# The last stage's attention rewritten: mask in PSUM, values spread ahead of the loop, two pairs of groups in work

## The chip, the cores and the metric

The kernel runs on one core of a Trainium2 chip. The metric is the device time of one execution in microseconds (us). Engines are named as the profile names them: PE is the matrix engine (PEld its weight loads), DVE the vector engine, ACT the scalar engine, POOL is GpSimd, SP issues the DMAs.

## What is computed

The reference is a two-layer perceiver with six blocks on `x` of 32 batches x 64 tokens x 128 (B, T, D). Only the last block is touched by the change. Seen by that block, S is the first axis (32, so the batches) and B the second (64, the tokens): attention runs over the 32 entries of the first axis, causally, separately for each of the 64 tokens, with 16 heads of 8 numbers and 4 key heads, each shared by 4 query heads.

```python
def _L1_ffn_ref(hidden_states, ln1_weight, ..., moe_w1, moe_w2):   # hidden_states = _layernorm(x)
    ln1_out = _layernorm(hidden_states, ln1_weight, ln1_bias)
    qkv = jnp.einsum('sbh,oh->sbo', ln1_out, qkv_weight)           # 16 query, 4 key, 4 value heads of 8
    k, v = jnp.repeat(k, 4, axis=2), jnp.repeat(v, 4, axis=2)
    scores = jnp.einsum('sbhd,tbhd->bhst', q, k) * scale
    scores = jnp.where(causal, scores, jnp.finfo(scores.dtype).min)
    probs = jax.nn.softmax(scores, axis=-1)
    attn = jnp.einsum('bhst,tbhd->sbhd', probs, v).reshape(S, B, H)
    hidden_after_attn = hidden_states + jnp.einsum('sbh,oh->sbo', attn, proj_weight)
    ln2_out = _layernorm(hidden_after_attn, ln2_weight, ln2_bias)
    ... # top 2 of 8 experts, F = 256, gelu
    return hidden_after_attn + moe_out
x = x + _L1_ffn_ref(_layernorm(x), ...)
```

## The kernel before

The program is a row of stages, each a block with one instruction list per engine, written out by hand with semaphores; a stage begins when the one before it has ended on all engines. The change is in the last stage but the final store, `stage_ffn1`. `x` lies in SBUF as 16 tiles (NT) of 128 rows; in the stages before, tile n holds 128 consecutive rows of (batch, token).

**Entry.** SP stores `x` to the output tensor, waits for it, and loads it back by token with four DMAs (`by_token`), so that partitions 32q to 32q+31 of tile n hold the 32 batches of token 4n+q; then it issues ten loads of weights. DVE waits for the reload (`ldx`), runs the first layer norm (`norm_vector`: L196 statistics, L199, L201, a power on POOL at L217, L205 the subtraction and scaling of each tile), then the second norm with gain and shift (L209, L211). PE transposes the result (L229), ACT copies it to `hT` (L237). PE makes queries and keys (L2640, L2641), which ACT copies to `QT` and `KT` (L2540, L2542), and the values of all tiles (L2643), which DVE copies to `V` (L2572).

**Loop.** A group g is one tile: 4 tokens, all 16 heads. The loop takes a pair of groups per turn, 8 turns, and an iteration starts with the scores of its own pair. Per group:

- POOL spreads the keys over heads (L2521: 128x2048 numbers, `kx`) and the values over the 4 tokens (L2526, `vx`); ACT copies the queries (L2548, `qs`).
- PE: scores, 4 matmuls on 32 columns of the array each, 512 wide (L2653).
- DVE: mask added (L2580, reads PSUM), maximum (L2583), subtraction (L2586), ACT the exponential (L2551), DVE the sum (L2590), reciprocal (L2593), multiplication (L2596), 32x32 transposes (L2600, `PT`).
- PE: probabilities times values for all heads and all key heads (L2660, 512 wide); DVE keeps the right key head (L2603), adds over key heads (L2608), transposes (L2611).
- PE transposes (L2665), ACT copies (L2555), PE projects (L2668), DVE adds to `hn` (L2614).

Buffers are double (`[a]` with a = g mod 2), and each engine goes through the steps for both groups of the pair before the next step. After the loop DVE adds `hn` to `x` (L2617), the third norm follows, the routing and the experts (`Moe`, L1356, L1365, L1383, L1397).

## Time and profile before

| | us |
|---|---|
| median of 3 runs | 3585.48 (3583.09 to 3586.24) |
| time of the profiled execution | 3584.38 |
| its span | 3582.6 |
| last stage, from the first DMA of `x` (3189.80) to the end | 392.8 |
| of it: until POOL's first key spread (3247.09) | 57.3 |
| of it: the 8 pairs, to the last add into `hn` (3427.30) | 180.2 |
| of it: from there to the end | 155.3 |

The profiled execution's time is 1.8 us above its span and 1.1 us below the median. A time such as 3247.09 is counted from the span's start. PE's fp32 matmuls stand in the records as two instructions each (x8 for 4 matmuls).

### The profile page before, as it was taken

The numbers are of one execution on the slowest core, as the hardware profiler recorded it, in microseconds if no ns is written. First come the engines' busy times: TensorE is split into PE (matmuls) and PEld (weight loads), VectorE is DVE, ScalarE is ACT, GpSimd is POOL, SyncE is SP. The second block draws the span as 40 slices with busy tenths as digits, with TensorE's granted clock in tenths as the row PEclk, the third lists the DMA queues.
The fourth block names the chain that finished last, engine by engine and source line by source line (L and its number), as shares of the span: only waits on it lengthen the run. The fifth ranks groups of instructions, "written<-read, shape, count | busy, mean of one in ns | idle before, by whom it ended". The sixth has DMA issues, their size and how long they took to land. (4 is left out here: it accounts for less than half of the span.)

```text
span 3582.6 us, 61448 instructions
## 1 busy us (share of the span) xinstructions
PE 3029.7 (85%) x19468; PEld 1775.1 (50%) x19468; DVE 2220.2 (62%) x4759; ACT 1464.9 (41%) x2290; POOL 1968.8 (55%) x1270
## 2 busy tenths in 40 slices
PE   4799999999995789958999999999994888834368
PEld 2455555555553767723444444444442777721146
DVE  4577777777774541156767767767736666545753
ACT  2466666666662223344444444444432121101123
POOL 2577777788775300026888888888870333323300
PEclk8899999999997899978999999999996999966679
DMA  5655555555530010010000000000000000020000
GB/s 171 165 187 190 188 180 178 182 186 186 188 139 3 0 48 0 0 43 19 28 27 23 23 27 27 18 27 27 19 0 8 1 0 0 0 52 0 0 1 12
DMA packets 143131, 230.56 MB, mean 64 GB/s; under 512 B 15683, under 2 KB 80779, under 8 KB 143052
## 3 DMA queue, kind: packets, MB, share of 16 engines
q1 hardware_dynamic: 143052, 229.55, 19.9%
q8 instruction: 44, 0.72, 0.1%
q14 instruction: 35, 0.29, 0.0%
HBM read 147.03 MB, written 82.47 MB: 64 GB/s over the span
## 5 line engine op out<-in xcount | busy, mean ns | idle before, releaser
L432 POOL TENSOR_TENSOR sb_a_acc<-sb_a_acc,sb_a_PT 128x1024 f32<-128x1024 f32 x256 | 604.4, 2361 | 36.7 <-ACT sb_a_PT L510 29.5
L593 DVE TENSOR_REDUCE sb_a_mx<-ps_a_A 128x1 f32<-128x512 f32 x768 | 506.4, 686 | 97.7 <-PE ps_a_A L752 92.6
L510 ACT ACTIVATE sb_a_PT<-ps_a_SC 128x1024 f32<-128x1024 f32 (+1 forms) x416 | 425.8, 1024 | 314.1 <-PE ps_a_SC L775 274.1
L1649 POOL TENSOR_TENSOR sb_a_acc<-sb_a_acc,sb_a_PT 128x512 f32<-128x512 f32 (+2 forms) x384 | 487.7, 1270 | 38.5 <-ACT sb_a_PT L1741 12.5
L1741 ACT ACTIVATE sb_a_PT<-ps_a_SC 128x1024 f32<-128x1024 f32 (+2 forms) x256 | 234.3, 916 | 561.2 <-PE ps_a_SC L2012 327.3
L2028 PE MATMUL ps_a_PV<-sb_a_PT,sb_a_XN 128*128 128x512 f32 (+2 forms) x896 | 433.1, 600 | 0.0
L1836 DVE TENSOR_REDUCE sb_a_mx<-ps_a_A 128x1 f32<-128x512 f32 x384 | 256.1, 679 | 266.0 <-PE ps_a_A L1987 265.6
L2012 PE MATMUL ps_a_SC<-sb_a_QX,sb_a_XT 128*128 128x512 f32 (+1 forms) x832 | 397.3, 597 | 0.0
L752 PE MATMUL ps_a_A<-sb_a_KS,sb_a_QS 97*128 97x512 bf16 x768 | 301.6, 393 | 24.1 <-DVE sb_a_QS L585 18.2
L786 PE MATMUL ps_a_PV<-sb_a_PT,sb_a_V 128*32 128x256 f32 (+1 forms) x3328 | 267.3, 393 | 5.6 <-ACT sb_a_PT L510 5.2
L775 PE MATMUL ps_a_SC<-sb_a_QS,sb_a_KS 105*128 105x128 bf16 (+1 forms) x3328 | 257.7, 220 | 13.4 <-DVE sb_a_QS L607 13.4
L775 PEld LDWEIGHTS ps_a_SC<-sb_a_QS,sb_a_KS 105*128 105x128 bf16 (+1 forms) x3328 | 218.1, 99 | 84.3 <-ACT sb_a_PT L510 23.2
L2012 PEld LDWEIGHTS ps_a_SC<-sb_a_QX,sb_a_XT 128*128 128x128 f32 (+1 forms) x832 | 152.6, 186 | 203.4 <-issue 200.4
L2028 PEld LDWEIGHTS ps_a_PV<-sb_a_PT,sb_a_XN 128*128 128x128 f32 (+2 forms) x896 | 163.1, 190 | 129.7 <-issue 116.6
L973 POOL TENSOR_TENSOR sb_a4c_LT<-sb_a4c_E,sb_LV 128x512 f32<-128x512 f32 x48 | 66.6, 1394 | 285.7 <-DVE sb_a4c_QL L1002 224.2
L217 POOL TENSOR_TENSOR sb_rstd<-sb_rstd,sb_half 128x16 f32<-128x16 f32 x8 | 23.2, 2906 | 350.0 <-DVE sb_rstd L201 350.0
L432 POOL TENSOR_TENSOR sb_a_acc<-sb_a_PT 128x1024 f32<-128x1024 f32 x32 | 75.4, 2357 | 227.3 <-ACT sb_a_PT L510 227.3
L1611 POOL TENSOR_TENSOR sb_a_XN<-sb_a_C,sb_a_gm 128x1536 f32<-128x1536 f32 x64 | 123.4, 1951 | 92.7 <-PE ps_a_PV L2028 89.3
L1830 DVE TENSOR_SCALAR sb_a_C<-sb_a_C,sb_a_cag,sb_a_crs 128x128 f32<-128x128 f32 (+1 forms) x416 | 170.7, 483 | 2.6 <-POOL sb_a_crs L1604 2.6
L752 PEld LDWEIGHTS ps_a_A<-sb_a_KS,sb_a_QS 97*128 97x128 bf16 x768 | 74.6, 97 | 175.0 <-DVE sb_a_mx L593 110.4
L1022 DVE TENSOR_TENSOR sb_a4c_XX<-sb_a4c_XX,ps_a4c_PP 128x1024 f32<-128x1024 f32 (+1 forms) x80 | 89.1, 1113 | 113.1 <-PE ps_a4c_PP L958 113.1
L1987 PE MATMUL ps_a_A<-sb_a_XTb,sb_a_QXb 128*128 128x512 bf16 x384 | 137.3, 386 | 16.3 <-DVE sb_a_mx L1836 16.3
(526 smaller groups left out, 5914.2 us busy)
## 6 DMA issues: line engine op xcount, KB each, us to landing
sb_a_C<-in_ctx_dram SPq DMA_DIRECT2D x64, 768.0 KB
...
sb_a_KS<-a_KD SPq DMA_DIRECT2D x256, 192.0 KB
...
sb_a_KS<-a_KD SPq DMA_DIRECT2D x256, 108.2 KB
...
```

Source lines behind the costliest of these rows:

```text
L432: pool.tensor_tensor(acc[:, :], first[:, :], PT[slot(a, j)][:, :], ALU.add).then_inc(s["acc"], 1)
L510: act.activation(PT[slot(a, j)][0:n, :], SC[(a + j) % 2][0:n, :], ACT.Exp).then_inc(s["exp"], 1)
L593: v.tensor_reduce(mx[:, p, c:c + 1], A[u % 2][:, :], AXX, ALU.max).then_inc(s["am"], 1)
L752: mm = pe.matmul(A[u % 2][:, :], QS[a][0:ROWM + 1, p, :], KS[a][0:ROWM + 1, p, 512 * c:512 * c + 512], start=True, stop=True)
L775: mm = pe.matmul(SC[(a + j) % 2][0:m, P * p:P * p + P], KS[a][0:ROWS, p, P * j:P * j + m], QS[a][0:ROWS, p, :], start=True, stop=True)
L786: mm = pe.matmul(PV[32 * g:32 * g + 32, 0, :], V[a][0:m, j, 32 * g:32 * g + 32], PT[slot(a, j)][0:m, G * T * g:G * T * g + G * T], start=( ...
L1649: pool.tensor_tensor(acc[a][0:m, :], first, PT[u % 4][0:m, HQ * i:HQ * i + HQ], ALU.add).then_inc(s["acc"], 1)
L1741: act.activation(PT[u % 4][0:m, 0:n], SC[u % 2][0:m, 0:n], ACT.Exp).then_inc(s["exp"], 1)
L1830: v.tensor_scalar(C[a][0:m, j, :], C[a][0:m, j, :], cag[a][0:m, j, 0:1], crs[a][0:m, j:j + 1], ALU.subtract, ALU.mult)\
L1836: v.tensor_reduce(mx[:, u % 4, u // 4:u // 4 + 1], A[u % 2][:, :], AXX, ALU.max).then_inc(s["am"], 1)
L2012: mm = pe.matmul(o, XT[a][:, col(j):col(j) + m], QX[a][:, :, :], start=True, stop=True)
L2028: mm = pe.matmul(PV[:, :], XN[a][0:m, j, :], PT[u % 4][0:m, HQ * i:HQ * i + HQ], start=(j == 0), stop=(j == NK))
```

## The change

**Entry.** `x` is stored as before, but DVE no longer waits for a reload: the first norm runs on `x` in its old order. The weights are issued right behind the store. When the first norm is done, SP stores `hn` to a scratch tensor and loads it by token into `HP`; `x` itself is reloaded by token after that. The second norm also runs in the old order; the reordering to tokens is made by ACT's copy into `hT`, whose writes are now 32 numbers apart, and PE's query and key matmuls wait for all four of these copies. DVE makes two small bf16 copies, the mask for 16 heads (`cmb`) and four unit matrices side by side (`rep4`).

**Values.** POOL clears a tile `vx` of 8192 numbers per partition between the powers of the first and the second norm. DVE writes the values into it from PSUM with 4 instructions, one per key head, each head's 8 numbers at their own place among 32 columns. V's copy and POOL's 16 spreads go.

**Loop.** POOL spreads 10 heads of the keys, ACT the other 6, with one instruction each; `kx` has four buffers, so both can be 4 groups ahead. ACT's copy of the queries goes. The mask enters the scores by a bf16 matmul over 32 rows that starts the accumulation, so DVE takes the maximum and the subtraction straight from PSUM. The exponentials are transposed undivided; the product with the values is made per key head, 16 matmuls of 128 columns into one 128-wide result, which needs no selection of key heads; DVE transposes it from PSUM and multiplies by the reciprocal sums there. The loops are unrolled.

```diff
+    HP = sb("HP", [P, NT, D])
+    HD = nc.dram_tensor("a5_HD", (B * T, D), F32, kind="Internal").ap()
...
+    vx = sb("vx", [P, NT, Q4, KVH, KD])
+    kx = [sb(f"kx{i}", [P, Q4, H, B]) for i in range(4)]
...
-            sp.wait_ge(s["st"], 16)
-            by_token = d["out"].rearrange("b (n q) d -> q b n d", q=Q4)
-            for q in range(Q4):
-                sp.dma_start(k.x[B * q:B * q + B, :, :], by_token[q]).then_inc(s["ldx"], 16)
...
+            sp.wait_ge(s["n"]["norm"], NT)
+            sp.dma_start(HD.rearrange("(n p) d -> p n d", p=P), k.hn[:, :, :]).then_inc(s["sth"], 16)
+            sp.wait_ge(s["sth"], 16)
+            by_token = HD.rearrange("(b n q) d -> q b n d", b=B, q=Q4)
+            for q in range(Q4):
+                sp.dma_start(HP[B * q:B * q + B, :, :], by_token[q]).then_inc(s["ldh"], 16)
...
+            pool.memset(vx[:, :, :, :, :], 0.0).then_inc(s["vz"], 1)
...
-            pool.wait_ge(s["vc"], 1)
-            with pool.Fori(0, NT // 2) as i:
...
-                    wait(pool, s["sc"], g - 1)
-                    pool.tensor_tensor(kx[a][:, :, :, :],
...
+            for g in range(NT):
+                wait(pool, s["sc"], g - 3)
+                pool.tensor_tensor(kx[g % 4][:, :, 0:KH, :], tok(KT, g).unsqueeze(2).to_broadcast([P, Q4, KH, B]),
+                                   k.heads[:, 0:KH].unsqueeze(1).unsqueeze(3).to_broadcast([P, Q4, KH, B]), ALU.mult).then_inc(s["kp"], 1)
...
-            norm_scalar(k, act, s["n1"], banks)
+            for c in range(NT // 4):
+                act.wait_ge(s["n1"]["turned"], c + 1)
+                act.activation(k.hT[:, :].rearrange("p (t b) -> p b t", b=B)[:, 8 * c:8 * c + 8, :],
+                               banks[c % 2][:, :].rearrange("p (b t) -> p b t", t=T), ACT.Copy).then_inc(s["n1"]["copied"], 1)
...
+            def spread(g):
+
+                wait(act, s["sc"], g - 3)
+                for h in range(KH, H):
+                    act.activation(kx[g % 4][:, :, h, :], tok(KT, g), ACT.Identity, scale=k.heads[:, h:h + 1]).then_inc(s["ka"], 1)
...
-            v.wait_ge(s["ldx"], 16 * Q4)
...
+            v.wait_ge(s["cm"], Q4 + 1)
+            v.tensor_copy(cmb[:, :, :], cmask[0:B, :].unsqueeze(1).to_broadcast([B, H, B])).then_inc(s["cb"], 1)
+            v.tensor_copy(rep4[:, :, :], k.ident[0:B, 0:B].unsqueeze(1).to_broadcast([B, Q4, B])).then_inc(s["cb"], 1)
...
-            v.tensor_copy(flat(V), LG[:, :]).then_inc(s["vc"], 1)
...
-                    v.tensor_tensor(Sm[a][:, :, :], hb(SB[a]), cmask[:, :].unsqueeze(1).to_broadcast([P, H, B]), ALU.add).then_inc(s["dm"], 1)
...
-                    v.tensor_tensor(Sm[a][:, :, :], Sm[a][:, :, :], mm_[a][:, :].unsqueeze(2).to_broadcast([P, H, B]), ALU.subtract)\
...
-                    v.tensor_tensor(Sm[a][:, :, :], Sm[a][:, :, :], mm_[a][:, :].unsqueeze(2).to_broadcast([P, H, B]), ALU.mult)\
...
-                    v.tensor_tensor(Om[a][:, :, :].rearrange("p (k h) q -> p k (h q)", k=KVH),
...
-                    v.tensor_reduce(R[a][:, :], Om[a][:, :, :].rearrange("p (k h) q -> p (h q) k", k=KVH), AXX, ALU.add).then_inc(s["r1"], 1)
...
+                cs = slice(DH * c, DH * c + DH)
+                v.tensor_tensor(vx[:, :, :, c, cs], values[:, :, cs].unsqueeze(2).to_broadcast([P, NT, Q4, DH]),
+                                k.quad[:, :].unsqueeze(1).unsqueeze(3).to_broadcast([P, NT, Q4, DH]), ALU.mult).then_inc(s["vc"], 1)
...
+            def tops(g):
+                wait(v, s["sc"], g + 1)
+                v.tensor_reduce(top[g % 2][:, :], hb(SB[g % 2]), AXX, ALU.max).then_inc(s["dx"], 1)
...
+            def less(g):
+                wait(v, s["dx"], g + 1)
+                v.tensor_tensor(Sm[g % 2][:, :, :], hb(SB[g % 2]), top[g % 2][:, :].unsqueeze(2).to_broadcast([P, H, B]), ALU.subtract)\
...
+            def sums(g):
+                wait(v, s["ex"], g + 1)
+                wait(v, s["nr"], g - 1)
+                v.transpose(flat(PT[g % 2]), flat(Sm[g % 2])).then_inc(s["pt"], 1)
+                v.tensor_reduce(sum_[g % 2][:, :], Sm[g % 2][:, :, :], AXX, ALU.add).then_inc(s["su"], 1)
...
+            def turn(g):
+                wait(v, s["pv"], g + 1)
+                v.transpose(R[g % 2][:, :], OB[g % 2][:, 0:P]).then_inc(s["r2"], 1)
...
+            def normalise(g):
+                wait(v, s["r2"], g + 1)
+                wait(v, s["rc"], g + 1)
+                r = R[g % 2][:, :].rearrange("p (h k d) -> p h k d", h=4, k=KVH)
+                by = sum_[g % 2][:, :].rearrange("p (k h) -> p h k", k=KVH).unsqueeze(3).to_broadcast([P, 4, KVH, DH])
+                v.tensor_tensor(r, r, by, ALU.mult).then_inc(s["nr"], 1)
...
+            def add(g):
+                wait(v, s["pr"], g + 1)
+                v.tensor_tensor(HP[:, g, :], HP[:, g, :], banks[g % 2][:, P:2 * P], ALU.add).then_inc(s["hx"], 1)
...
+            for i in range(NT // 2):
+                now, then = (2 * i, 2 * i + 1), [g for g in (2 * i + 2, 2 * i + 3) if g < NT]
+                for g in then:
+                    tops(g)
+                for g in then:
+                    less(g)
+                for g in now:
+                    turn(g)
+                for g in now:
+                    normalise(g)
+                for g in then:
+                    sums(g)
+                for g in then:
+                    inverse(g)
+                for g in now:
+                    add(g)
...
-            v.tensor_tensor(k.x[:, :, :], k.x[:, :, :], k.hn[:, :, :], ALU.add).then_inc(s["xh"], 1)
+            v.wait_ge(s["ldx"], 16 * Q4)
+            v.tensor_tensor(k.x[:, :, :], k.x[:, :, :], HP[:, :, :], ALU.add).then_inc(s["xh"], 1)
...
-                pe.wait_ge(s["n1"]["copied"], c + 1)
+                pe.wait_ge(s["n1"]["copied"], NT // 4)
...
+            def scores(g):
+                wait(pe, s["kp"], g + 1)
+                wait(pe, s["ka"], (H - KH) * (g + 1))
+                wait(pe, s["ds"], g - 1)
+                o = SB[g % 2]
+                pe.matmul(o[:, :], rep4[:, :, :], cmb[:, :, :], start=True, stop=False)
+                q = tok(QT, g)
+                for t in range(Q4):
+                    mm = pe.matmul(o[B * t:B * t + B, :], q[:, t, :], kx[g % 4][:, t, :, :], start=False, stop=True)
+                mm.then_inc(s["sc"], 1)
+
+            def products(g):
+                wait(pe, s["pt"], g + 1)
+                wait(pe, s["r2"], g - 1)
+                for c in range(KVH):
                     for t in range(Q4):
-                        mm = pe.matmul(SB[a][B * t:B * t + B, :], qs[a][:, B * t:B * t + B], kx[a][:, t, :, :], start=True, stop=True)
-                    mm.then_inc(s["sc"], 1)
-                for a, g in gs:
-                    wait(pe, s["pt"], g + 1)
-                    wait(pe, s["vx"], g + 1)
...
+                        mm = pe.matmul(OB[g % 2][B * t:B * t + B, 0:P], vx[:, g, t, c, :], PT[g % 2][:, 4 * c:4 * c + 4, :],
+                                       start=(c == 0), stop=(c == KVH - 1))
+                mm.then_inc(s["pv"], 1)
...
+                wait(pe, s["nr"], g + 1)
+                wait(pe, s["zc"], g - 1)
+                pe.transpose(banks[g % 2][:, 0:P], R[g % 2][:, :], k.ident[:, :]).then_inc(s["zt"], 1)
+
+            def project(g):
...
+            for i in range(NT // 2):
+                now = (2 * i, 2 * i + 1)
+                for g in now:
+                    products(g)
+                for g in (2 * i + 4, 2 * i + 5):
+                    if g < NT:
+                        scores(g)
+                for g in now:
+                    turn(g)
+                for g in now:
+                    project(g)
```

PE in the loop before, from an iteration's first scores to its end (`sb_a_qs`, `sb_a_kx` queries and keys, `sb_a_PT` probabilities, `sb_a_R` the turned result, `sb_a_zs` its copy):

```order
L2653 MATMUL ps_a5m_U<-sb_a_kx,sb_a_qs 32x512 x4
L34 REGISTER_ALU x2
L2653 MATMUL ps_a5m_U<-sb_a_kx,sb_a_qs 32x512 x4
L2660 MATMUL ps_a5m_U<-sb_a_PT,sb_a_vx 32x512 x8
L2665 MATMUL ps_a5m_D<-sb_ident,sb_a_R 128x128 x2
L2668 MATMUL ps_a5m_D<-sb_a_WpT,sb_a_zs 128x128 x2
L2646 REGISTER_ALU
L2646 COMPARE_AND_BRANCH
```

PE in the loop of the change, from the last two scores of one turn to the first scores of the next:

```order
L2701 MATMUL ps_a5m_U<-sb_a_cmb,sb_a_rep 128x512
L2704 MATMUL ps_a5m_U<-sb_a_kx,sb_a_QT 32x512 x4
L2701 MATMUL ps_a5m_U<-sb_a_cmb,sb_a_rep 128x512
L2704 MATMUL ps_a5m_U<-sb_a_kx,sb_a_QT 32x512 x4
L2719 MATMUL ps_a5m_D<-sb_ident,sb_a_R 128x128 x2
L2724 MATMUL ps_a5m_D<-sb_a_WpT,sb_a_zs 128x128 x2
L2712 MATMUL ps_a5m_U<-sb_a_PT,sb_a_vx 32x128 x32
L2701 MATMUL ps_a5m_U<-sb_a_cmb,sb_a_rep 128x512
L2704 MATMUL ps_a5m_U<-sb_a_kx,sb_a_QT 32x512 x4
```

The scores of the pair after the next now stand between the products and the transposes of this pair, each behind its mask matmul; a pair's products are 32 matmuls of a quarter of the width, where they were 8.

DVE in the loop before, one iteration up to the second transposes:

```order
L2580 TENSOR_TENSOR sb_a_Sm<-ps_a5m_U,sb_a_cmask 128x512
L34 REGISTER_ALU
L2580 TENSOR_TENSOR sb_a_Sm<-ps_a5m_U,sb_a_cmask 128x512
L2583 TENSOR_REDUCE sb_a_mm<-sb_a_Sm 128x16 x2
L2586 TENSOR_TENSOR sb_a_Sm<-sb_a_Sm,sb_a_mm 128x512 x2
L2590 TENSOR_REDUCE sb_a_mm<-sb_a_Sm 128x16 x2
L2593 RECIPROCAL sb_a_mm<-sb_a_mm 128x16 x2
L2596 TENSOR_TENSOR sb_a_Sm<-sb_a_Sm,sb_a_mm 128x512 x2
L2600 STREAM_TRANSPOSE sb_a_PT<-sb_a_Sm 128x512 x2
L2603 TENSOR_TENSOR sb_a_Om<-ps_a5m_U,sb_subhead 128x512 x2
L2608 TENSOR_REDUCE sb_a_R<-sb_a_Om 128x128 x2
L2611 STREAM_TRANSPOSE sb_a_R<-sb_a_R 128x128 x2
```

DVE in the loop of the change, one whole turn:

```order
L2610 TENSOR_REDUCE sb_a_top<-ps_a5m_U 128x16 x2
L2614 TENSOR_TENSOR sb_a_Sm<-ps_a5m_U,sb_a_top 128x512 x2
L2629 STREAM_TRANSPOSE sb_a_R<-ps_a5m_U 128x128 x2
L2636 TENSOR_TENSOR sb_a_R<-sb_a_R,sb_a_sum 128x128 x2
L2620 STREAM_TRANSPOSE sb_a_PT<-sb_a_Sm 128x512
L2621 TENSOR_REDUCE sb_a_sum<-sb_a_Sm 128x16
L2620 STREAM_TRANSPOSE sb_a_PT<-sb_a_Sm 128x512
L2621 TENSOR_REDUCE sb_a_sum<-sb_a_Sm 128x16
L2625 RECIPROCAL sb_a_sum<-sb_a_sum 128x16 x2
L2640 TENSOR_TENSOR sb_a_HP<-sb_a_HP,ps_a5m_D 128x128 x2
```

Gone are the mask's addition, the multiplication of 128x512, the selection and the sum over key heads; the maximum and the subtraction of the next pair now stand ahead of this pair's transposes, and the add into `HP` is last.

POOL from the norms' powers into the loop, before:

```order
L217 TENSOR_TENSOR sb_rstd<-sb_rstd,sb_half 128x16 x2
L2517 UNCONDITIONAL_BRANCH
L2517 ISA
L2521 ISA
L2521 TENSOR_TENSOR sb_a_kx<-sb_a_KT,sb_heads 128x2048
L34 REGISTER_ALU
L2521 ISA
L2521 TENSOR_TENSOR sb_a_kx<-sb_a_KT,sb_heads 128x2048
L2526 ISA
L2526 TENSOR_TENSOR sb_a_vx<-sb_a_V,sb_quad 128x128
```

POOL from the block's first instruction to its last, in the change (x16 are all 16 groups):

```order
L2520 MEMSET sb_a_cmask 128x32
L2523 AFFINE_SELECT sb_a_cmask<-sb_a_cmask 32x32 x4
L217 TENSOR_TENSOR sb_rstd<-sb_rstd,sb_half 128x16
L2527 MEMSET sb_a_vx 128x8192
L217 TENSOR_TENSOR sb_rstd<-sb_rstd,sb_half 128x16
L2532 TENSOR_TENSOR sb_a_kx<-sb_a_KT,sb_heads 128x4x320 x16
L217 TENSOR_TENSOR sb_rstd<-sb_rstd,sb_half 128x16
```

The clearing of `vx` stands directly behind the power of the first norm; in the loop only the key spreads are left.

## Rows read from the trace of the kernel before

**Rows 1.** Windows of the last stage: entry and loop; columns in the first row.

```profile
core 0: us, PE busy (x) PEld busy (x) DVE busy (x) ACT busy (x) POOL busy (x), PEclk, DMA share, GB/s
3189.80:3247.10 57.30, 16.21 (x68) 10.84 (x68) 22.80 (x103) 8.30 (x18) 6.75 (x8) 0.59 0.31 81
3247.10:3427.30 180.20, 69.00 (x304) 19.31 (x304) 123.27 (x176) 17.62 (x46) 67.19 (x32) 0.60 0.00 0
```

**Rows 2.** Timeline of the loop, one iteration (its scores start at 3297.55).

```profile
3297.55 3.64 PE L2653 MATMUL ps_a5m_U<-sb_a_kx,sb_a_qs 128*32 128x512 f32 x16
3299.70 7.67 POOL L2521 TENSOR_TENSOR sb_a_kx<-sb_a_KT,sb_heads 128x2048 f32<-128x2048 f32 x2 [6.41 <-PE ps_a5m_U L2653]
3301.87 1.27 DVE L2583 TENSOR_REDUCE sb_a_mm<-sb_a_Sm 128x16 f32<-128x512 f32 x2
3303.06 4.86 DVE L2586 TENSOR_TENSOR sb_a_Sm<-sb_a_Sm,sb_a_mm 128x512 f32<-128x512 f32 x2
3309.21 0.37 DVE L2593 RECIPROCAL sb_a_mm<-sb_a_mm 128x16 f32<-128x16 f32 x2
3310.70 1.30 DVE L2600 STREAM_TRANSPOSE sb_a_PT<-sb_a_Sm 128x512 f32<-128x512 f32 x2
3317.60 0.49 DVE L2611 STREAM_TRANSPOSE sb_a_R<-sb_a_R 128x128 f32<-128x128 f32 x2
3317.96 0.56 PE L2665 MATMUL ps_a5m_D<-sb_ident,sb_a_R 128*128 128x128 f32 x2 [2.89 <-DVE sb_a_R L2611]
3318.96 0.51 ACT L2548 ACTIVATE sb_a_qs<-sb_a_QT 128x128 f32 x2
3319.60 0.29 DVE L2614 TENSOR_TENSOR sb_hn<-sb_hn,ps_a5m_D 128x128 f32 x1 [1.51 <-PE ps_a5m_D L2668]
3319.81 2.84 PE L2653 MATMUL ps_a5m_U<-sb_a_kx,sb_a_qs 128*32 128x512 f32 x16
```

**Rows 3.** Instructions of three lines: duration ns min/median/max, first and last start.

```profile
L2586 DVE TENSOR_TENSOR sb_a_Sm<-sb_a_Sm,sb_a_mm x16: 680/1638/4116, 3258.3 to 3414.0; 128x512 f32<-128x512 f32 x16
L2580 DVE TENSOR_TENSOR sb_a_Sm<-ps_a5m_U,sb_a_cmask x16: 691/692/692, 3253.0 to 3411.6; 128x512 f32<-128x512 f32 x16
L2521 POOL TENSOR_TENSOR sb_a_kx<-sb_a_KT,sb_heads x16: 3629/3634/4082, 3247.1 to 3392.5; 128x2048 f32<-128x2048 f32 x16
```

**Rows 4.** Timeline of the entry.

```profile
3202.53 3.19 DVE L196 BATCH_NORM_STATS2 sb_st<-sb_x 128x6 f32<-128x128 f32 x16 [15.93 <-DMA sb_x<-out_dram]
3210.08 4.19 DVE L205 TENSOR_SCALAR sb_hn<-sb_x,sb_mv,sb_rstd 128x128 f32<-128x128 f32 x16 [3.09 <-POOL sb_rstd L217]
3242.29 3.65 PE L2643 MATMUL ps_a_L<-sb_a_WkvT,sb_hT 128*128 128x32 f32 x32
3242.49 0.60 ACT L2542 ACTIVATE sb_a_KT<-ps_a5m_U 128x512 f32<-128x512 f32 x1 [0.26 <-PE ps_a5m_U L2641]
```

**Rows 5.** Timeline of an earlier stage's entry, with the same norm.

```profile
2701.74 7.41 DVE L205 TENSOR_SCALAR sb_hn<-sb_x,sb_mv,sb_rstd 128x128 f32<-128x128 f32 x16 [3.02 <-POOL sb_rstd L217]
2701.92 3.51 POOL L2163 MEMSET sb_a_KP<- 128x4096 f32 x1
```

**Rows 6.** Window of the entry's transfers; columns as in rows 1.

```profile
3196.00:3210.20 14.20, 0.00 (x0) 0.00 (x0) 4.55 (x34) 0.00 (x0) 2.90 (x1) 0.50 1.00 250
```

**Rows 7.** PE where passes are short, at the full clock (stages one and last).

```profile
1002.69 0.64 PE L786 MATMUL ps_a_PV<-sb_a_PT,sb_a_V 128*32 128x256 f32 x8
1003.49 0.61 PE L775 MATMUL ps_a_SC<-sb_a_QS,sb_a_KS 105*128 105x128 bf16 x8
3462.98 1.95 PE L1365 MATMUL ps_a5m_D<-sb_a_W,sb_a5m_H 128*128 128x128 f32 x16
```

**Rows 8.** Window of an earlier stage's loop; columns as in rows 1.

```profile
2800.00:2844.00 44.00, 37.87 (x271) 33.16 (x271) 28.89 (x40) 8.29 (x17) 14.18 (x10) 0.92 0.00 1
```

**Rows 9.** Groups on ACT in the stage two before: busy, mean ns, idle before.

```profile
L1700 ACT ACTIVATE sb_a_XT<-ps_a_M,sb_ident,sb_a_keep 128x512 f32<-128x512 f32 x124 | 85.0, 685 | 0.0
L1741 ACT ACT_TABLE_LOAD x1 | 1.3, 1283 | 0.0
```

More of the change, by code:

```diff
@@ L2503, in _ @@
             sp.dma_start(W2[:, :, :], d["L1_ffn_moe_w2"].rearrange("e (f p) d -> p (e f) d", p=P)).then_inc(s["ldw"], 16)
+            sp.wait_ge(s["n"]["norm"], NT)
[4 more added lines that the diff above has]
+                sp.dma_start(HP[B * q:B * q + B, :, :], by_token[q]).then_inc(s["ldh"], 16)
+            sp.wait_ge(s["st"], 16)
+            by_token = d["out"].rearrange("b (n q) d -> q b n d", q=Q4)
+            for q in range(Q4):
+                sp.dma_start(k.x[B * q:B * q + B, :, :], by_token[q]).then_inc(s["ldx"], 16)
         @block.gpsimd
@@ new lines, in inverse @@
+            def inverse(g):
+                wait(v, s["su"], g + 1)
+                v.reciprocal(sum_[g % 2][:, :], sum_[g % 2][:, :]).then_inc(s["rc"], 1)
+            def turn(g):
[7 more added lines that the diff above has]
+                v.tensor_tensor(r, r, by, ALU.mult).then_inc(s["nr"], 1)
@@ new lines, in add @@
+            def add(g):
+                wait(v, s["pr"], g + 1)
+                v.tensor_tensor(HP[:, g, :], HP[:, g, :], banks[g % 2][:, P:2 * P], ALU.add).then_inc(s["hx"], 1)
+            for f in (tops, less, sums, inverse):
+                for g in range(2):
+                    f(g)
+            v.wait_ge(s["ldh"], 16 * Q4)
+            for i in range(NT // 2):
[14 more added lines that the diff above has]
+                    add(g)
@@ new lines, in _ @@
+            pe.wait_ge(s["vc"], KVH)
+            pe.wait_ge(s["cb"], 2)
+            def scores(g):
[8 more added lines that the diff above has]
+                mm.then_inc(s["sc"], 1)
@@ new lines, in project @@
+            def project(g):
+                wait(pe, s["zc"], g + 1)
+                wait(pe, s["hx"], g - 1)
+                pe.matmul(banks[g % 2][:, P:2 * P], zs[g % 2][:, :], WpT[:, :], start=True, stop=True).then_inc(s["pr"], 1)
+            for g in range(4):
+                scores(g)
+            for i in range(NT // 2):
+                now = (2 * i, 2 * i + 1)
+                for g in now:
+                    products(g)
+                for g in (2 * i + 4, 2 * i + 5):
+                    if g < NT:
+                        scores(g)
+                for g in now:
+                    turn(g)
+                for g in now:
+                    project(g)
```

116 lines of the change are left out of this document (33 added, 83 removed).

## The prediction

> **What bounds the kernel now.** I read the page, then windows over the last stage, then the timeline of the entry and of one loop iteration, and the groups of instructions. The change lies in the last 392.8 us of a span of 3582.6; all that stands before 3189.80 stays. In the loop no engine is full: over 180.2 us DVE works 123.3, PE 69.0, POOL 67.2, ACT 17.6, with PE's granted clock at 0.60 [rows 1]. The timeline shows why. One iteration runs as a single chain: scores at 3297.55, DVE's maxima at 3301.87, subtractions, sums, transposes to 3312.0, the wide products, selection, second transposes at 3317.60, PE's transposes, ACT's copies, projections, adds, and the next scores at 3319.81. That is 22.26 us a turn, 8 times [rows 2]. Within it, two subtractions take 4.86 us instead of 1.3, because they meet POOL's key spreads (7.67 us from 3299.70): the fastest is 0.68 us, the slowest 4.12, while L2580, with one operand in PSUM, never leaves 0.69 [rows 2, 3]. So the bound is a chain of latencies with DVE as its largest member, and a rewrite gains where it shortens DVE's list and lets one pair's chain lie under another's.
>
> **The entry.** DVE's first statistics start at 3202.53, 12.7 us after the stage's start, having waited for the reload of `x`; in the change they start at about 3189.9. To the end of the last L205 (3214.27) the first norm takes 11.7 us [rows 4]. New behind its power is POOL's clearing of 8192 numbers. The trace holds the same situation once: L205's 16 instructions took 7.41 us beside a memset of 4096 numbers (3.51 us), against 4.19 without [rows 4, 5]. So the memset cost 3.2 us, nearly its whole length, and one of twice the size (7.0 us) costs between 0 and 7.0; I take 6.5. The norm then ends at 3189.9 + 11.7 + 6.5 = 3208.1. DVE next waits for the weights. Reload and weights filled the DMA engines for 14.2 us before [rows 6]; now the store of `x` stands in the reload's place from 3190.3 on, so they land by about 3204.5, hidden behind the memset. Without the memset's block the wait for them would keep all but 3.6 us.
> From L205's end to the last copy into `KT` (3243.09) it is 28.8 us [rows 4]. I add 0.7 for the two bf16 copies and 0.9 for PE's wait for all four copies into `hT` (it started after three); that these copies write 32 numbers apart has no row, 0 to 0.6 us each, and I take 0. POOL's first spread then starts at 3208.1 + 30.4 + 0.2 = 3238.7 instead of 3247.1: 8.4 us earlier. The values reach `vx` by 4 DVE instructions of about 0.61 after L2643, at 3244, so PE's first scores wait for them and not for POOL. The store of `hn`, its reload and the reload of `x` are some 3 MB at 250 GB/s [rows 6], 12 us behind PE's and DVE's preparation and loop; if that cover failed, the wait would stand ahead of the first add only.
>
> **The loop: DVE per pair.** By pace in the rows: maxima 1.2 (3301.87 to 3303.06), subtractions from PSUM 1.2, transposes 1.2, sums 1.2, reciprocals 0.3, small transposes 0.45, the two new multiplications of 128x128 at the pace of L2614 0.5, adds 0.5 [rows 2]. Sum 6.55, and 0.4 for waits between steps: 7.0 us. Gone are the mask's addition, the wide multiplication, the selection, the sum over key heads and the blocked subtraction.
>
> **PE per pair.** Sixteen records of scores, two groups, take 3.64 us at the 1.2 GHz level: four rounds of 0.855 and an end of 0.2 [rows 2]. So a group costs 1.71, or 0.85 at 2.4 GHz. The mask matmul is 512 bf16 columns; eight passes of 128 took 0.61 [rows 7], so 0.2 to 0.3, I take 0.25 (0.45 at 1.2). The new products of a group are eight rounds of four passes of 128 columns. From below they cost what the wide ones did, 0.85; two rounds of 256 columns took 0.64 with their end [rows 7], so a round of 128 lies under 0.16, and I take 0.15: 1.2 us a group. Transposes, ACT's copies and projections took 1.85 at 1.2 GHz (3317.96 to 3319.81) [rows 2], about 1.2 at 2.4. PE's turn is 2 x 1.2 + 2 x 1.1 + 1.2 = 5.8 at 2.4 GHz, under DVE's 7.0, and 2 x 1.71 + 2 x 2.16 + 1.85 = 9.6 at 1.2 GHz, over it. A loop in which PE was busy 37.87 of 44 us had a clock of 0.92 [rows 8]; the old one, busy 69 of 180, had 0.60. With 5.8 of 7.0 I expect mostly 2.4 GHz, with a third of the turns at 1.2.
>
> **ACT and POOL per pair.** ACT: 12 key spreads at the pace of two L2548 in 0.51 (0.21 each, at most 0.3), two exponentials, two copies: 4.2 to 5.3 us, hidden. Identity beside Exp needs no table load: the stage two before runs both, 124 times on L1700, with one load at its Exp [rows 9]. POOL: 1280 of 2048 numbers, 3.63 x 10/16 = 2.3 us each [rows 3], 4.6 a pair, hidden but for the lock below.
>
> **Sum.** The first turn ends late: PE has the scores of groups 4 and 5 ahead of the first transposes, and group 5's keys are POOL's sixth: 6 x 2.3 + 1.2 + 2.2 (transposes to adds) = 17.2; the first multiplication can meet a spread for 2.3 more: 19.5. Six turns of 7.0 are 42, the last 3.5: 65. A third of the turns at 1.2 GHz adds 5, the first scores at that level 2: **72 us**, between 60 and 96. The loop's end moves from 3427.3 to 3238.7 + 72 = 3310.7. The rest, 155.3, stays. Minus 116.6 from the profiled 3584.38 is 3467.8; the median of the runs is 1.1 above: **3469 us**.
>
> **Rivals.**
> - *Short passes have a floor (0.15).* Eight un-tiled passes of 128 columns took 0.61 [rows 7], 0.076 each; if 32 tiled ones cannot be closer, a group's products take 2.4 and PE's turn is 8.2: about 1.2 more on seven turns, **3477**. Against it: four tiled weight loads leave no gap between rounds now, 3.64 for four rounds of 0.855 [rows 2]. The Trainium skill, "TensorE: Matmul & The Clock Gate", section on the back-to-back issue gap, gives about 81 ns per load-and-matmul pair at 128 columns; by it a group takes 2.6, PE's turn 8.6, and the time would be 3480. No row shows it for tiled passes.
> - *PE stays at 1.2 GHz (0.14).* Turns of 9.6, fill 24, end 5: loop 87, **3484**. For it: the old loop's 0.60. Against it: at that level PE would be busy nearly always, as where the clock was 0.92.
> - *DVE waits for POOL in every turn (0.12).* The new multiplication has both operands in SBUF, like L2586. POOL's next spread starts when the scores are done, about 2.2 us after the subtraction; the multiplication stands at 1.7 to 2.2. One block a turn is 2.1 x 6 = 13, **3482**; two, or blocked transposes, 25, **3494**. Maxima beside a spread ran unblocked (1.27 for two at 3301.87), but L205, with one SBUF tensor, was blocked by a memset [rows 2, 5]; transposes beside POOL have no row. The Trainium skill, "SBUF — State Buffer", "Who interferes with whom", says that a DVE instruction with one SBUF input outside the 2-port modes does not contend; by it the transposes stay free, and only the multiplication is at risk.
> - *Column groups take turns (0.06).* 32 passes at the 0.122 of L1365 (16 in 1.95 [rows 7]) are 3.9 a group; PE's turn 11.2, **3498**.
> - *Slower (0.01).* Successive key heads add into the same PSUM columns; if each pass waited for the end of the one before (0.107 + 0.22), a group took 10.5, the turn 24.5, the loop 191: **3588**. It decides from 0.32 us a pass on. Against it: L1365 also adds twice into one place at 0.122.
> - *The memset hardly blocks (0.06).* DVE waits for the weights instead: 3465; with no turn at 1.2 GHz as well, **3458**.
>
> **Numbers.** The forecast's own case (products hidden, clock mostly high, lock rare) has 0.44, from 3458 to 3477. Range: from 3453 (fill of 17, no turn at 1.2 GHz, memset free, none of the 0.4 a turn) to 3496, which leaves out the last two costly cases and part of the third. What is left, 0.02, is code fetched for the unrolled loop and the like. This kernel can be told apart at 0.2%, 7 us; the gain is 3.2%, so faster 0.98, same 0.01, slower 0.01.
>
> **What would show it.** The first norm's statistics right at the stage's start; L205 near 10.7 us beside a memset of 7; adds into `HP` 7 us apart per pair, DVE with hardly an idle moment in the middle turns, PE's granted clock over 0.8 there; a product group of 32 records near 1.4 us. Wrong would be: records of products over 2 us a group, multiplications over 2 us, a clock near 0.5, or table loads on ACT.

## The result, and the profile of the changed kernel

The changed kernel takes 3458.27 us (median of 4 runs, 3455.61 to 3471.53) against 3585.86 (3583.09 to 3588.47) on the same chip: 0.9652 of the time, 95% interval 0.9626 to 0.9678. The forecast was 3469 (3453 to 3496). The profiled execution took 3456.78, its span is 3455.0. The windows of its last stage, entry, loop and middle turns, columns as in [rows 1]:

```profile
3186.29:3234.73 48.44, 12.74 (x45) 7.62 (x45) 28.93 (x104) 9.26 (x17) 13.59 (x9) 0.61 0.58 139
3234.73:3299.73 65.00, 54.63 (x729) 28.29 (x728) 53.46 (x132) 40.56 (x128) 37.19 (x16) 0.87 0.01 2
3257.50:3295.00 37.50, 32.66 (x532) 18.05 (x534) 37.50 (x95) 26.16 (x83) 16.25 (x7) 0.98 0.01 2
```

Against [rows 1] the entry fell from 57.3 to 48.4 us and the loop from 180.2 to 65.0; the 155.3 us behind the loop are the same. The span fell by 127.6; 3.5 of them are not the change's: all that stands before the stage, identical code, ended 3.5 us earlier in this execution. Over the loop VectorE's busy time fell from 123.3 to 53.5 us. In the middle turns it is busy in 37.50 of 37.50 us, and TensorE's granted clock is 0.98. One such turn from the timeline (start, duration, engine, line):

```profile
3270.07 0.48 DVE L2640 TENSOR_TENSOR sb_a_HP<-sb_a_HP,ps_a5m_D 128x128 f32<-128x128 f32 x2
...
3270.16 1.95 PE L2712 MATMUL ps_a5m_U<-sb_a_PT,sb_a_vx 128*32 128x128 f32 x64
3270.47 1.28 DVE L2610 TENSOR_REDUCE sb_a_top<-ps_a5m_U 128x16 f32<-128x512 f32 x2
3271.67 1.27 DVE L2614 TENSOR_TENSOR sb_a_Sm<-ps_a5m_U,sb_a_top 128x512 f32<-128x512 f32 x2
...
3272.80 1.06 PE L2704 MATMUL ps_a5m_U<-sb_a_kx,sb_a_QT 128*32 128x512 f32 x8
3272.86 0.50 DVE L2629 STREAM_TRANSPOSE sb_a_R<-ps_a5m_U 128x128 f32<-128x128 f32 x2
...
3273.29 0.45 DVE L2636 TENSOR_TENSOR sb_a_R<-sb_a_R,sb_a_sum 128x128 f32<-128x128 f32 x2
...
3273.97 4.66 POOL L2532 TENSOR_TENSOR sb_a_kx<-sb_a_KT,sb_heads 128x1280 f32<-128x1280 f32 x2 [1.63 <-PE ps_a5m_U L2704]
...
3276.35 0.49 DVE L2640 TENSOR_TENSOR sb_a_HP<-sb_a_HP,ps_a5m_D 128x128 f32<-128x128 f32 x2
```

The adds return after 6.28 us, where one iteration took 22.26 [rows 2]. Two things to see: 64 product passes (two records for each of a pair's 32 matmuls) in 1.95 us, 30 ns each; and the multiplications L2636 end at 3273.74, 0.23 us before GpSimd, released by the scores, starts its next spread. In [rows 2] the subtractions stood inside such a spread. The entry, by the same view, with the clearing beside the first norm and the first two of the regrouping copies:

```profile
3193.76 6.92 POOL L2527 MEMSET sb_a_vx<- 128x8192 f32 x1
3193.85 10.56 DVE L205 TENSOR_SCALAR sb_hn<-sb_x,sb_mv,sb_rstd 128x128 f32<-128x128 f32 x16 [3.09 <-POOL sb_rstd L217]
...
3204.44 0.23 DVE L2592 COPY sb_a_Wpp<-sb_a_Wpr 128x128 f32<-128x128 f32 x1
...
3222.64 1.92 ACT L2545 ACTIVATE sb_hT<-ps_a5m_D 128x512 f32<-128x512 f32 x2 [16.00 <-PE ps_a5m_D L229]
```

The first turn and the last, by the same view. The last products run while the granted clock is back at 1.2 GHz, from 3293.4 to 3296.9:

```profile
3234.73 13.87 POOL L2532 TENSOR_TENSOR sb_a_kx<-sb_a_KT,sb_heads 128x1280 f32<-128x1280 f32 x6 [22.24 <-ACT sb_a_KT L2551]
...
3249.39 1.94 PE L2704 MATMUL ps_a5m_U<-sb_a_kx,sb_a_QT 128*32 128x512 f32 x8
...
3251.10 2.60 PE L2712 MATMUL ps_a5m_U<-sb_a_PT,sb_a_vx 128*32 128x128 f32 x64
...
3294.05 3.30 PE L2712 MATMUL ps_a5m_U<-sb_a_PT,sb_a_vx 128*32 128x128 f32 x64
```

### The profile page after: what moved, and what is told of

Its sections match the earlier page's. It is cut to its first block and busy times, and to the rows that moved or that the text cites. A ratio compares the mean times of both kernels' runs of the same rounds, so it can differ in the third digit from the quotient of the medians.

```text
span 3455.0 us, 62037 instructions
## 1 busy us (share of the span) xinstructions
PE 3009.0 (87%) x19821; PEld 1782.9 (52%) x19868; DVE 2156.4 (62%) x4716; ACT 1489.7 (43%) x2370; POOL 1947.5 (56%) x1255
## 5 line engine op out<-in xcount | busy, mean ns | idle before, releaser
L928 ACT ACTIVATE sb_a4c_T1s<-ps_a4c_T 128x512 f32<-128x512 f32 x80 | 47.8, 597 | 245.2 <-PE ps_a4c_T L949 245.2
```

## The experiments

Each starts from the changed kernel. Its ratio is to the kernel before on the same chip. A total is a weak measure of a few us here: in the profiled executions the last stage's first statistics started between 3182.36 and 3197.59, behind code that was never edited. So small effects are read as **the stretch** from these statistics (L196) to the addition of the loop's output onto `x`, within one trace. It is 113.4 us in the changed kernel, and 114.8 when it ran again. Its part **behind the values** starts with the first of VectorE's four value passes (L2605).

> The changed kernel unchanged, beside the runs that follow on the same chip. Both theories: 3458 us as before, the last stage 113.4 us from its first statistics to the addition of the attention onto x, turns of 6.28 us, where the earlier stages alone move the total by several us from run to run.

Measured: 3456.15 us (5 runs), 0.966 (0.9644 to 0.9676); turns of 6.28. The 1.4 us more lie between the copy of `WkT` and the values (17.65 against 16.20): TensorE's clock rose 8.4 us behind that copy, 2.9 us into the projections, where it had risen 3.9 us behind it, ahead of them. This part is the stretch's noise, and 1.4 us is not the most of it: in the runs below that leave the entry alone it took 16.20 to 19.76 us. Behind the values the changed kernel took 62.2 and 62.1 us, and three runs with edits in the entry alone 62.1 to 62.3 (only with the old entry it was 61.1). So edits of the loop are read there.

**The mask back on VectorE.**

```diff
+                v.tensor_tensor(Sm[g % 2][:, :, :], hb(SB[g % 2]), cmask[:, :].unsqueeze(1).to_broadcast([P, H, B]), ALU.add).then_inc(s["dm"], 1)
...
-                v.tensor_tensor(Sm[g % 2][:, :, :], hb(SB[g % 2]), top[g % 2][:, :].unsqueeze(2).to_broadcast([P, H, B]), ALU.subtract)\
+                v.tensor_tensor(Sm[g % 2][:, :, :], Sm[g % 2][:, :, :], top[g % 2][:, :].unsqueeze(2).to_broadcast([P, H, B]), ALU.subtract)\
...
-                pe.matmul(o[:, :], rep4[:, :, :], cmb[:, :, :], start=True, stop=False)
```

> The mask goes back onto VectorE (an add of 128x512 from PSUM into SBUF for each group, then the maximum and the difference from SBUF); TensorE's mask passes are gone. Theory A, VectorE's list paces the turns: the changed kernel's turns are 6.28 us with VectorE always busy, and the add costs 0.64 each, so a turn is 7.6 and the time 3458 + 8 x 1.28 = 3468 us. Theory B, on top of A the difference, now with both inputs in SBUF, is held up while GpSimd spreads keys (its 128x512 took 2.4 to 2.7 us in the kernel before, where it should be 0.64): up to 2 x 1.8 us a turn more, 3468 to 3497 us, to be seen as a long difference in the trace. Theory C, something else paces the turns (GpSimd, TensorE, the chain through all engines): 3458 us, VectorE's idle time fills up.

Measured: 3484.5 us, 0.9725 (0.9709 to 0.9742); stretch 141.5, behind the values 86.7 against 62.2. The timeline of two turns shows why:

```profile
3276.33 3.43 DVE L2620 TENSOR_TENSOR sb_a_Sm<-sb_a_Sm,sb_a_top 128x512 f32<-128x512 f32 x2
3276.55 5.41 POOL L2532 TENSOR_TENSOR sb_a_kx<-sb_a_KT,sb_heads 128x1280 f32<-128x1280 f32 x2 [5.88 <-PE ps_a5m_U L2711]
...
3280.11 2.20 DVE L2642 TENSOR_TENSOR sb_a_R<-sb_a_R,sb_a_sum 128x128 f32<-128x128 f32 x2
...
3289.07 4.69 POOL L2532 TENSOR_TENSOR sb_a_kx<-sb_a_KT,sb_heads 128x1280 f32<-128x1280 f32 x2 [7.11 <-PE ps_a5m_U L2711]
3289.24 4.67 DVE L2642 TENSOR_TENSOR sb_a_R<-sb_a_R,sb_a_sum 128x128 f32<-128x128 f32 x2
...
3293.84 0.70 DVE L2626 STREAM_TRANSPOSE sb_a_PT<-sb_a_Sm 128x512 f32<-128x512 f32 x1
```

Turns are 11.3 to 11.6 us while GpSimd has keys to spread and 7.39 once it has none (3307.77 to 3315.16). Theory A's pass costs 1.11 us a turn (7.39 against 6.28) where I had put 1.28, and B's mechanism comes on top, 3.9 us a turn. It takes the difference as named: in the first turn above one of the two waits, 3.43 us instead of 1.28, and so it is in three of the four turns in which GpSimd spreads (3.43 each; the very first pair's took 3.70). One multiplication waits behind it, 2.20 us for two instead of 0.45. In the second turn above the difference was through before GpSimd started (1.28), and both multiplications waited: 4.67 us. There GpSimd starts 0.17 us before them; in the changed kernel 0.23 us after their end.

**One pair in work.**

```diff
-            for f in (tops, less, sums, inverse):
-                for g in range(2):
-                    f(g)
...
-                now, then = (2 * i, 2 * i + 1), [g for g in (2 * i + 2, 2 * i + 3) if g < NT]
...
+                now = (2 * i, 2 * i + 1)
+                for f in (tops, less, sums, inverse, turn, normalise, add):
+                    for g in now:
+                        f(g)
```

> One pair of groups in work: VectorE finishes a pair (maximum to sum into the output) before the next pair's maximum, TensorE turns and projects before the scores ahead. Theory A, the overlap hides the chain from the normalised product over TensorE, ScalarE and TensorE back to VectorE and the wait for exponential and products: by the first turn's rows some 2.5 us a turn, so turns of about 8.8 us and 3458 + 20 = 3478 us. Theory B, TensorE is also left idle enough for its clock to fall to 1.2 GHz, as in the kernel before's loop: another 2.5 us a turn, about 3498 us, granted clock in the loop under 0.7. Theory C, the overlap is worth little against the shorter list: under 3463 us.

Measured: 3485.14 us, 0.9721 (0.97 to 0.9743); stretch 141.9, behind the values 89.2. ScalarE's and TensorE's lists are reordered to match. Six turns in one window, columns as in [rows 1]:

```profile
3261.60:3323.50 61.90, 43.51 (x530) 20.78 (x528) 40.05 (x97) 26.38 (x83) 18.78 (x8) 0.83 0.01 1
```

Turns are 10.3 us: VectorE works 6.7 of them and waits 3.6, TensorE's clock is 0.83. Between A (8.8) and B (11.3), of both kinds. The multiplications are not blocked (0.45). The overlap is worth 4.0 us a turn, the clock that goes with it included.

**GpSimd spreads all heads.**

```diff
-    KH = 10
+    KH = 16
```

> GpSimd spreads all 16 heads of the keys, ScalarE none. By size a spread is 16/10 of 2.33 us = 3.73 us, a pair 7.5 us, over VectorE's 6.28. Theory A, GpSimd becomes the bound and nothing else happens: turns of 7.5 us (+10 over eight), the first turn some 4 to 5 us longer, together about 3472 us. Theory B, a GpSimd that is never idle also holds up VectorE's passes that read two operands from SBUF (multiplication by the reciprocal sums), and these then hold up the turn: turns of 9 us or more, 3485 us or more, with multiplications of over 1 us in the trace where they are 0.23 now. Theory C, GpSimd's share is not near the path: 3458 to 3462 us.

Measured: 3476.05 us, 0.97 (0.9683 to 0.9718); stretch 130.2, behind the values 77.5. Turns are 10.9 us while spreads run, as in this one, then 6.2 to 7.8:

```profile
3269.35 14.56 POOL L2532 TENSOR_TENSOR sb_a_kx<-sb_a_KT,sb_heads 128x2048 f32<-128x2048 f32 x4
...
3275.27 5.14 DVE L2636 TENSOR_TENSOR sb_a_R<-sb_a_R,sb_a_sum 128x128 f32<-128x128 f32 x2
...
3280.96 0.64 DVE L2621 TENSOR_REDUCE sb_a_sum<-sb_a_Sm 128x16 f32<-128x512 f32 x1
...
3281.52 0.69 DVE L2620 STREAM_TRANSPOSE sb_a_PT<-sb_a_Sm 128x512 f32<-128x512 f32 x1
```

Theory B's mechanism: both multiplications wait. The total is nearer to A's, since only the first turn and two more were of this kind. Sums and transposes of the same length as before run beside the spreads.

**Products in another order.**

```diff
-                for c in range(KVH):
-                    for t in range(Q4):
+                for t in range(Q4):
+                    for c in range(KVH):
```

> The 32 product passes of a group in another order: the eight key heads of one row quarter follow one another, instead of the four row quarters of one key head. Output and number of passes are the same. Theory A, the passes are short (30 ns each) because neighbours go to four different quarters of the array and run side by side: passes to one quarter then follow one another, 1.95 us per pair become up to 7.8, TensorE needs up to 10.4 us a turn and paces it: up to 3458 + 8 x 4.1 = 3491 us. Theory B, the passes are short of themselves: same time, 3458 us, same 1.95 us.

Measured: 3474.54 us, 0.9691 (0.967 to 0.9713); stretch 127.7, behind the values 76.4. In the turn's timeline the same 64 passes take 2.2 times as long, TensorE is busy 7.94 of 8.2 us at the full clock and sets the turn:

```profile
3279.49 4.33 PE L2712 MATMUL ps_a5m_U<-sb_a_PT,sb_a_vx 128*32 128x128 f32 x64
...
3283.86 0.32 DVE L2629 STREAM_TRANSPOSE sb_a_R<-ps_a5m_U 128x128 f32<-128x128 f32 x1 [1.35 <-PE ps_a5m_U L2712]
```

Theory A, at half its price: 68 ns a pass when neighbours share a quarter (the 32 columns of the array that belong to one token), 30 when they don't.

**The old entry in front of the new loop.** Store, reload and only then the first norm, as in [rows 4].

```diff
+            v.wait_ge(s["ldx"], 16 * Q4)
             norm_vector(k, v, s["n"])
...
-            v.wait_ge(s["ldh"], 16 * Q4)
```

> The changed kernel with the entry of the kernel before: x is stored and read back regrouped before the first norm, the first norm works on the regrouped rows, its output is where the loop adds, and the copies of the turned norm are contiguous again. The loop is the changed kernel's. Theory A, the entry is worth what its rows say: statistics 13 us later (15.93 us of idle time instead of 2.93), copies and wait some 1.9 us shorter, so 11 us longer than the changed kernel, about 3469 us, and the loop keeps its turns of 6.28 us. Theory B, the gain of the entry is taken up elsewhere (the weights end later than the norm): under 3463 us. Theory C, the loop depends on the phase it is entered with: turns of 10 to 11 us and 3485 us or more.

Measured: 3475.44 us, 0.9699 (0.9665 to 0.9734). From the last instruction of the stage before (L2341) to the addition it is 127.80 us against 116.65: 11.15 more, theory A. That is not the 8.9 us by which the entry got shorter, since this is not quite the old entry: the clearing stays and still holds up L205 (10.56 us). The timeline shows the wait again:

```profile
3205.18 3.19 DVE L196 BATCH_NORM_STATS2 sb_st<-sb_x 128x6 f32<-128x128 f32 x16 [16.44 <-DMA sb_x<-out_dram]
```

**The clearing late**, after the second norm's first transposes.

```diff
-            pool.memset(vx[:, :, :, :, :], 0.0).then_inc(s["vz"], 1)
             norm_pool(k, pool, s["n1"])
+            pool.wait_ge(s["n1"]["turned"], 1)
+            pool.memset(vx[:, :, :, :, :], 0.0).then_inc(s["vz"], 1)
```

> GpSimd clears the spread values' buffer only after the first transposes of the second norm, when VectorE has nothing to do, instead of beside the first norm's application. Theory A, the clearing of 6.92 us holds up VectorE's 16 passes (10.56 us instead of 4.19) and this is all on the path: the entry is 6.4 us shorter, about 3452 us. Theory B, the weights' loads end the wait right behind the first norm (by the rows of before they land some 11.7 us after the stage's statistics begin at the earliest, 15 at the latest): VectorE then waits for them and 3 us or less are gained, 3455 us or more. Theory C, the phase of the loop shifts and GpSimd's spreads begin to hold up VectorE's multiplications, as they do with the mask on VectorE: 3480 us or more, turns of 11 us.

Measured: 3463.81 us, 0.9666 (0.9637 to 0.9694); stretch 114.5. Theory B, as the timeline shows:

```profile
3199.56 4.19 DVE L205 TENSOR_SCALAR sb_hn<-sb_x,sb_mv,sb_rstd 128x128 f32<-128x128 f32 x16 [3.09 <-POOL sb_rstd L217]
...
3209.30 0.23 DVE L2593 COPY sb_a_Wpp<-sb_a_Wpr 128x128 f32<-128x128 f32 x1 [5.55 <-DMA sb_a_W<-in_L_ffn_moe_w_dram]
```

The norm is 6.37 us shorter and the weights take 5.55 of it back: they land 17.3 us behind the first statistics, the blocked norm had ended at 18.1. The second norm's transposes start 34.3 us behind the statistics, not 35.2; the stretch hides these 0.9 in its noise.

**Clearing and weights' wait both late.**

```diff
-            v.wait_ge(s["ldw"], 16 * 10)
-            v.tensor_copy(Wpp[:, :, :, :], Wpr[:, :].rearrange("p (k h d) -> p h k d", k=KVH, h=4)).then_inc(s["wk"], 1)
...
+            v.wait_ge(s["ldg"], 16 * 4)
             norm_vector(k, v, s["n1"], k.hn, Y, g1, b1)
+            v.wait_ge(s["ldw"], 16 * 6)
+            v.tensor_copy(Wpp[:, :, :, :], Wpr[:, :].rearrange("p (k h d) -> p h k d", k=KVH, h=4)).then_inc(s["wk"], 1)
```

> The clearing is moved as before, and VectorE waits for the norm's own parameters alone ahead of the second norm; its wait for the other weights and the copy of the projection weight stand behind that norm. Theory A, the clearing was free only because VectorE had to wait for the weights' loads anyway (5.55 us in the run with the late clearing), so both waits have to go: norm ends 6.4 us earlier, some 1 us comes back by weight transposes that stand in the way later, so the stretch of 113.4 us becomes 108 to 109 and the total about 3453 us. Theory B, the loads of the norm's parameters land as late as the rest (all are issued together): no change or 1 us, the idle time then stands ahead of the second norm's statistics.

Measured: stretch 110.1, that is 3.4 to 4.8 less, where theory A said 108 to 109. The second norm follows the first without a wait, and its transposes start 30.0 us behind the first statistics instead of 35.2:

```profile
3203.54 3.16 DVE L196 BATCH_NORM_STATS2 sb_st<-sb_hn 128x6 f32<-128x128 f32 x16
...
3221.28 1.97 PE L229 MATMUL ps_a5m_D<-sb_ident,sb_a_Y 128*128 128x128 f32 x8
```

The total does not show it: 3458.45 us (3444.81 to 3464.58), 0.9651 (0.9625 to 0.9677), against 3456.15 of the changed kernel beside it.

**The wait for the values late**, ahead of the first products.

```diff
-            pe.wait_ge(s["vc"], KVH)
...
             for g in range(4):
                 scores(g)
+            pe.wait_ge(s["vc"], KVH)
```

> TensorE waits for VectorE's four value passes only ahead of the first products, not ahead of the first scores. Theory A: the first scores start when the first keys are spread, some 2.5 to 3 us earlier, the first pair is finished 2 to 3 us earlier, turns stay 6.28 us: about 3455 us. Theory B, GpSimd's next spreads are then released earlier against VectorE's multiplications by the reciprocal sums (both operands in SBUF) and hold them up, as in the run with the mask on VectorE (4.7 us for two instead of 0.45): turns of 10 to 11 us, 3475 us or more. Theory C: the first pair is paced by something else, no change.

Measured: 3459.02 us, 0.9655 (0.963 to 0.968); stretch 113.4, no change, but not by theory C. The first scores came earlier and at 2.4 GHz, GpSimd then ran its first ten spreads without a pause, and the first multiplications met them (3.20 us instead of 0.45). The first add still came 1.5 us sooner behind the first spread. The next turn gave that back: it took 7.7 us, with its multiplications free (0.45), and VectorE waited 1.46 us for projections that stood behind scores at 1.2 GHz. So it is A's gain, less B's block in one turn, less a turn with a slow clock. The timeline:

```profile
3245.19 23.20 POOL L2532 TENSOR_TENSOR sb_a_kx<-sb_a_KT,sb_heads 128x1280 f32<-128x1280 f32 x10 [22.24 <-ACT sb_a_KT L2551]
...
3248.22 1.07 PE L2703 MATMUL ps_a5m_U<-sb_a_kx,sb_a_QT 128*32 128x512 f32 x8
...
3260.67 3.20 DVE L2636 TENSOR_TENSOR sb_a_R<-sb_a_R,sb_a_sum 128x128 f32<-128x128 f32 x2
...
3274.18 0.51 DVE L2640 TENSOR_TENSOR sb_a_HP<-sb_a_HP,ps_a5m_D 128x128 f32<-128x128 f32 x2 [1.46 <-PE ps_a5m_D L2723]
```

**Passes without use, to hold the clock.**

```diff
+            for _ in range(24):
+                pe.matmul(SB[0][:, :], k.ident[:, :], W1[:, 0:2, :], start=True, stop=True)
             norm_tensor(k, pe, s["n1"], banks, Y)
...
+            for _ in range(4):
+                pe.matmul(OB[0][:, :], k.ident[:, :], W1[:, 0:2, :], start=True, stop=True)
             pe.wait_ge(s["vc"], KVH)
```

> 28 passes of 128x512 whose results nobody reads are added on TensorE in its idle time, 24 ahead of the second norm's transposes and 4 between the projections and the first scores. Theory A, the first turn is long (23.2 us) partly because TensorE stands at 1.2 GHz for 12 us of it, after 2.6 idle us ahead of the first scores: at 2.4 GHz the first scores take 1.4 us instead of 2.5 and the first products 1.0 less, so the stretch of 113.4 us becomes 109 to 111, total about 3455 us. Theory B, the first turn is paced by the spreads and VectorE, or the clock falls all the same in the idle moments between the first scores: no change. Theory C, with faster scores GpSimd's spreads are released earlier and hold up the first multiplications, as with the later wait for the values: 3.2 us instead of 0.45 in the first turn, which eats the gain.

Measured: 3458.9 us, 0.9666 (0.9651 to 0.9682), no gain. The passes overran: the transposes started 7.8 us after the copy of `WkT`, not at once, and the stretch became 119.3. Behind the values it was 61.3 us to the addition against 62.2. The gain isn't where I had looked for it. The first multiplication started 14.1 us behind the values instead of 16.5, so the clock's part of the first turn is real; but it was blocked (theory C), and the first add came 0.8 us later than in the changed kernel. The 0.9 us lie in the last pair, where the clock held at 2.4 GHz until 3302.7: 2.40 us between its add and the one before instead of 4.0. The timeline:

```profile
3254.44 4.03 DVE L2636 TENSOR_TENSOR sb_a_R<-sb_a_R,sb_a_sum 128x128 f32<-128x128 f32 x2
...
3297.29 1.95 PE L2716 MATMUL ps_a5m_U<-sb_a_PT,sb_a_vx 128*32 128x128 f32 x64
```

**Both of the last ideas together** (16 passes ahead of the weights' transposes).

> The two changes together: clearing and weights' wait late, and passes without use that keep TensorE's clock (16 ahead of the weights' transposes, 4 ahead of the first scores). Theory A for both: 104 to 107 us instead of 113.4, total about 3450 us. Theory B for both: 113 us, 3458 us.

Measured: 3458.81 us, 0.9663 (0.9643 to 0.9683); stretch 117.1, longer than either theory said. The passes delayed the weights' transposes into the late clearing, and a copy of 128x128 that takes 0.22 us elsewhere had to sit it out, as the timeline shows:

```profile
3224.96 7.03 DVE L2600 COPY sb_a_WkT<-sb_a_WkvT 128x128 f32<-128x128 f32 x1 [5.40 <-ACT sb_a_WkvT L2542]
3224.99 6.93 POOL L2529 MEMSET sb_a_vx<- 128x8192 f32 x1 [14.51 <-PE ps_a5m_D L229]
```

**Two of the four regrouping copies on VectorE.**

```diff
-            for c in range(NT // 4):
+            for c in range(0, NT // 4, 2):
                 act.wait_ge(s["n1"]["turned"], c + 1)
...
+            for c in range(1, NT // 4, 2):
+                v.wait_ge(s["n1"]["turned"], c + 1)
+                v.tensor_copy(k.hT[:, :].rearrange("p (t b) -> p b t", b=B)[:, 8 * c:8 * c + 8, :],
+                              banks[c % 2][:, :].rearrange("p (b t) -> p b t", t=T)).then_inc(s["n1c"], 1)
```

> VectorE, which has nothing to do then, takes the second and fourth of the four regrouping copies from ScalarE. Theory A, the copies' 0.96 us each (0.60 without the stride) are on the path between transposes and projections: from the first transpose to the first projection 5.42 us become about 4.2. Theory B, the transposes set that time: no change. Either way 1 us or less in the total, so it is to be read in the trace.

Measured: one run, 3459.64 us; from first transpose to first projection 5.41 us as before. VectorE's copies took 1.04 and 1.01, and the transposes at 1.2 GHz set the pace up to the last copy, which stands ahead of the projections in both: theory B.

## Why the prediction was right, and where its sizes were off

The steps held: the entry is shorter because the reload left its head, VectorE's list is the bound of the middle turns, one pair's chain lies under the other's list. 11.0 us separate the forecast's 3467.8 from the profiled 3456.78:

- *All before stays*: 3.5 us, a spread between executions, outside the change.
- *The entry*: 48.4 us against 48.9. The memset's block, taken at 6.5, was 6.37. The weights, which I had landing 14.7 us behind the start, took 17.3 in the run that shows it, so without the block only 0.8 us are won and not the 3.6 I allowed. From L205's end to the first spread it is 30.3 against 30.6, and here errors cancel. From the first transpose to the first projection it took 5.42 us instead of 3.57, so 1.85 more where I had 0.9: the strided copies, taken at 0, cost 1.04 each (two that overlap show as 1.92) where one of 128x512 takes 0.60 in [rows 4]. The two bf16 copies cost 0.5 instead of 0.7, and a clock that had risen at 3225.2, before the projections, gave 0.9 back. That was luck: in the same kernel's second execution it rose later.
- *The fill*: 22.7 us to the first add, against 21.5 with the slow scores. The size is near, but the path I added it up from is not the one in the trace. GpSimd's sixth spread ended at 3248.6, and the scores that need it started at 3255.3; the first multiplications met no spread (0.45 us, not 2.3 more). What held the turn up was TensorE: the scores of groups 0 to 3 ran at 1.2 GHz, 2.5 us each, with the first products queued behind the last two until 3251.1.
- *Six turns of 7.0*: 37.7 us instead of 42. Between the steps on VectorE there was no wait at all (I had 0.4), and the two multiplications went at 0.39 of pace, the adds at 0.40, where I had 0.5 for each. The product group took 0.97 us, at the lower end of 0.85 to 1.28.
- *A third of the turns at 1.2 GHz, 5 us*: **the largest miss, 0 in these six turns.** The clock rose at 3252.5 and stayed until 3293.4. TensorE is busy 5.65 of 6.3 us in a turn, denser than the 5.8 of 7.0 I had counted; that this is why the clock held, no run shows.
- *The last*: 4.6 instead of 3.5. The clock fell at 3293.4, and the last products took 3.30 us instead of 1.95. In the run with the unused passes, where it held, the part took 2.9.

-3.5 - 0.5 + 1.2 - 4.3 - 5.0 + 1.1 = -11.0.

Of the rivals, "DVE waits for POOL in every turn" has the right mechanism: two runs switch it on turn after turn, three more in the first turn. With the mask on VectorE it cost 3.9 us a turn (11.3 against 7.39), near the 4.2 that I had for two blocks, and it did not last for six turns, since GpSimd works ahead and its spreads ran out. What decides is where I had looked: I put the multiplications 1.7 to 2.2 us behind the subtractions' start and the spread at 2.2; they stand at 1.6 to 2.1 and 2.3. It missed by 0.23 us, and nothing in the kernel guards that distance. The short-pass floor is refuted for passes on four quarters in turn (30 ns a pass). By the Trainium skill, "TensorE: Matmul & The Clock Gate", "Back-to-back issue gap", it would be about 81 ns a pass; this trace does not agree. Column groups do run side by side, and serial passes into the same PSUM columns cost 68 ns, far from the 0.32 us where that rival would decide. That TensorE stays at 1.2 GHz was true for the fill, and for 3.4 us at the end.

By experiment, read behind the values and with the runs' own side effects in them, the overlap of pairs is worth 27 us of the loop's 115 (89.2 against 62.2), the mask in PSUM 24 (86.7; its passes 9, the lock that they bring in the rest), ScalarE's share of the spreads 15 (77.5), the order of the products 14 (76.4). These don't add up to the whole: no two were switched together, and in the first three the granted clock fell as well, to 0.80 to 0.83 while the turns were long. What the loop owes to the spread values, to the missing selection and to the clock alone I didn't isolate.
